# Filling the second half's row regions with pad rows inside the attention loop, ten block places a tile

## The reference

```
x = x + attention(layernorm(x), key, value, adj)     # x: 4096 x 512, adj: 4096 x 4096 of 0 and 1
x = x + experts(layernorm(x))                         # 8 experts of 512 x 512, the best 2 for each row

attention: q = x Wq' + bq; k = key Wk' + bk; v = value Wv' + bv
           s = (q k' / sqrt(4096)) * adj ; entries under 1e-5 in size become -1e9
           out = softmax(s) v Wm' + bm
experts:   gate = softmax(x Wg + bg); the two largest, scaled to sum 1
           out = sum over those two of gate * (We[e] x + be[e])
```

## Time and profile before

| | us |
|---|---|
| median of 3 runs | 1821.15 |
| the runs | 1818.61 to 1823.14 |
| the profiled execution | 1816.43 |
| its span | 1814.7 |
| PE busy | 1785.6 (98%) |
| DVE busy | 1201.1 (66%) |
| ACT busy | 743.6 (41%) |
| POOL busy | 242.8 (13%) |

### The profile page before, as it was taken

How to read it: one execution, slowest core, us unless ns; L and a number is a source line. 1 busy time by engine, 2 the same in 40 slices (tenths; PEclk the granted TensorE clock), 3 DMA queues, 4 the chain that set the end, 5 groups by cost and what they waited for, 6 DMA issues and landing times.

```text
span 1814.7 us, 33108 instructions
## 1 busy us (share of the span) xinstructions
PE 1785.6 (98%) x8770; PEld 838.5 (46%) x8770; DVE 1201.1 (66%) x3200; ACT 743.6 (41%) x1445; POOL 242.8 (13%) x285
## 2 busy tenths in 40 slices
PE   8999999999999999999999999999999999899997
PEld 3455444444444444444444444444444444445553
DVE  6888766666666666666767666666666665465453
ACT  4444444444444434444443333333334443233343
POOL 2000000000000000000000000000000000145654
PEclk9999999999999999999999999999999999999999
DMA  6555455776667776666776655565555667899986
GB/s 210 167 189 188 156 134 137 163 171 164 162 169 165 162 168 156 166 158 156 169 165 163 152 144 136 140 139 135 134 139 131 145 156 174 201 308 240 185 157 82
DMA packets 428619, 296.63 MB, mean 163 GB/s; under 512 B 319249, under 2 KB 335633, under 8 KB 428562
## 3 DMA queue, kind: packets, MB, share of 16 engines
q1 hardware_dynamic: 389810, 230.36, 51.6%
q0 software_dynamic: 16864, 38.35, 10.9%
q10 hardware_dynamic: 21888, 27.27, 5.0%
HBM read 152.68 MB, written 67.72 MB: 121 GB/s over the span
## 4 chain that ended last, share of the span: by engine, by line
PE 91%; DVE 3%; issue 3%; DMA 1%; ACT 1%; POOL 1%; DVEq 0%; ACTq 0%; SPq 0%; POOLq 0%
PE ps L1466 18%; PE ps L1467 18%; PE ps L1468 18%; PE ps L1579 12%; PE ps L1580 12%; PE ps L1581 12%; PE ps L1651 1%; PE ps L1523 1%; DMA slots<-work,slots_u 1%; DVE work L1418 1%; PE ps L1589 0%; DVE work L1410 0%; ACT work L910 0%; POOL out L640 0%; DVEq L1414 0%
## 5 line engine op out<-in xcount | busy, mean ns | idle before, releaser
L1466 PE MATMUL ps<-key_region,work 128*128 128x512 f16 (+1 forms) x1336 | 506.9, 379 | 4.0 <-issue 2.5
L1467 PE MATMUL ps<-key_region,work 128*128 128x512 f16 (+1 forms) x1336 | 506.8, 379 | 0.0
L1468 PE MATMUL ps<-key_region,work 128*128 128x512 f16 (+1 forms) x1336 | 506.7, 379 | 0.0
L780 ACT ACTIVATE work<-work 128x512 f32<-128x512 f32 x256 | 161.3, 630 | 566.7 <-DVE work L1090 566.3
L1579 PE MATMUL ps<-val_region,work 128*128 128x512 f16 x1024 | 388.9, 380 | 4.0 <-DMA work<-work 2.8
L1580 PE MATMUL ps<-val_region,work 128*128 128x512 f16 x1024 | 389.1, 380 | 0.0
L1581 PE MATMUL ps<-val_region,work 128*128 128x512 f16 x1024 | 389.0, 380 | 0.0
L1090 DVE SCALAR_TENSOR_TENSOR work<-ps,r_cur,work 128x512 f32<-128x512 f32 x256 | 191.7, 749 | 147.5 <-PE ps L1468 133.2
L1112 DVE TENSOR_TENSOR work<-work 128x512 f16<-128x512 f32 x256 | 176.4, 690 | 71.9 <-ACT work L793 71.8
L1100 DVE CUSTOM_DVE_ANT_0 work<-work 128x512 f32<-128x512 f32 x256 | 177.3, 692 | 49.5 <-DVE work L1097 49.5
L788 ACT ACTIVATE work<-work,exp_bias 128x512 f32<-128x512 f32 x256 | 181.4, 709 | 61.2 <-DVE exp_bias L1108 54.6
(11 more groups left out here) (200 smaller groups left out, 1594.4 us busy)
## 6 DMA issues: line engine op xcount, KB each, us to landing
work<-in_adj SPq DMA_DIRECT2D x256, 256.0 KB, 2.9
val_region<-slots SPq DMA_DIRECT2D x58, 257.0 KB, 5.2
work<-in_valueT SPq DMA_DIRECT2D x8, 1024.0 KB, 6.7
work<-in_x SPq DMA_DIRECT2D x8, 1024.0 KB, 5.2
work<-in_keyT SPq DMA_DIRECT2D x8, 1024.0 KB, 5.5
q_scratch<-work SPq DMA_DIRECT2D x8, 1024.0 KB, 5.1
work<-q_scratch SPq DMA_DIRECT2D x32, 256.0 KB, 2.7
work<-in_x SPq DMA_DIRECT2D x32, 256.0 KB, 3.0
```

What stands on the lines that cost most here:

```text
L780: nc.scalar.activation(w[:, c * CW:(c + 1) * CW], s_adj[:, c % 2, :], ACT.Abs).then_inc(abs_done, 1)
L1466: nc.tensor.matmul(bank, st[0], mv[0], start=(k == 0), stop=False)
L1467: nc.tensor.matmul(bank, st[0], mv[1], start=False, stop=False)
L1468: last = nc.tensor.matmul(bank, st[1], mv[0], start=False, stop=(k == n - 1))
```

## The change

`slots[1]` gets 160 blocks instead of 137, and all of it is filled with pads ahead of the scatters into it. In iterations 2 to 17 SP issues ten more transfers of one block each: two after adjacency chunk 7 and two after each of the transposes 4 to 7. The eight pads of the second half behind the tables go, and with them the wait for them; in its place SP waits for the tables. POOL waits for all 160 fills before it scatters the first row of the second half. The setup transfers that wrote the second half's spare block now go to an unused place of `slots[0]`.

```diff
+    FILL = 10
+    assert FILL * TH > DUMMY + 2 and FILL % 5 == 0
...
-        slots = [nc.dram_tensor(f"slots{h}", ((DUMMY + 1) * P, ROW), F32, kind="Internal").ap() for h in range(HALVES)]
+        slots = [nc.dram_tensor(f"slots{h}", (FILL * TH * P, ROW), F32, kind="Internal").ap() for h in range(HALVES)]
...
+            def fill_slots(t, i):
+
+                for j in range(2):
+                    sp.dma_start(slots[1][bass.ds(t * (FILL * P) + (2 * i + j) * P, P), :], pad_row[:, :]).then_inc(filled, 16)
...
                 adjacency(t, 7)
+                if h == 0:
+                    fill_slots(t - 2, 0)
                 for c in range(ADJ, C):
                     turn_probs(t - 1, c)
+                    if h == 0:
+                        fill_slots(t - 2, c - ADJ + 1)
                     if not last and c < C - 1:
                         adjacency(t + 1, c - ADJ)
...
             def pad_regions(h):
 
+                if h:
+                    return
                 sp.wait_ge(tables_done, h + 1)
...
             pad_regions(1)
             sp.wait_ge(slotted, 32 * T)
-            sp.wait_ge(padded[1], 16 * E)
+            sp.wait_ge(tables_done, 2)
             for st in rest:
                 load_block(st)
...
-                    nc.gpsimd.dma_start(slots[h][DUMMY * P + q * rows:DUMMY * P + (q + 1) * rows, :], pad_row[part, :]
+                    nc.gpsimd.dma_start(slots[0][(DUMMY + 2 * h) * P + q * rows:(DUMMY + 2 * h) * P + (q + 1) * rows, :], pad_row[part, :]
                                         ).then_inc(y_added[8 * h + 2 * q + 1], 16)
...
                 scatter_rows(t, 0)
+            pool.wait_ge(filled, 16 * FILL * TH)
             with pool.Fori(TH, T - 2) as t:
```

More of the change, by code:

```diff
@@ L372, in graph_attention_moe_kernel @@
         padded = [sem(f"padded{h}") for h in range(HALVES)]
+        filled = sem("filled")
         tok_loaded = [sem(f"tok_loaded{b}") for b in range(TOKS)]
```

## The result

| | before | after |
|---|---|---|
| median of 20 runs each, us | 1819.32 | 1823.85 |
| lowest to highest | 1813.17 to 1823.38 | 1819.87 to 1832.46 |
| ratio after to before | | 1.0028, 95% interval 1.0019 to 1.0038 |
| span of the profiled execution | 1814.7 | 1822.6 |

The change makes the kernel slower by about 5.1 us (0.28%, interval 3.5 to 6.9 us). That is just inside the 0.3% that the prediction called no change, and outside zero: with 20 runs of each the difference shows.

What follows compares the result with a forecast made beforehand. The prediction took PE to bound the kernel from end to end. Its terms, 0 - 0 + 0.4 = +0.4 us, added to the expected median 1821.15, gave 1821.5 us, range 1817 to 1831.

Steps and rivals of the forecast that it cites:

- The step to 0 in fifteen iterations: Attention loop: q lands 4.1 us after issue, at most 4.3, PE needs it at 4.61; cost 0 in fifteen iterations.
- The hole in SP's queue has 8 us of cover: Block stage: the block loaded after the late pads arrives 8.0 us before PE turns it; removing the pads gains 0.
- The load of q is the transfer with the least room, 4.61 us from issue to use: Loop: q, issued at 644.25 and used at 648.86, decides the cost; other transfers behind the fills have more room.
- Two fills ahead are 1.4 us of data: Loop: the pair behind transpose 7 takes 2 x 0.70 = 1.4 us, with q's data behind it.
- It isn't delayed: SP after transpose 7: two fills take about 1 us, end at about 643.75, and q still goes at 644.25.
- At most 4.3 us: Loop: upper landing of q after issue in fifteen iterations, 2.9 + 1.4, against PE's need at 4.61.
- A share of 0.86: Transfer engines in the loop's iterations with fills: the share goes from 0.69 to 0.86.
- 0.4 us once, in the first iteration: First iteration: q lands at 3.6 + 1.4 = 5.0 us, so PE waits 0.4 us once.
- ACT's weight pieces are covered: Loop, another queue: a piece comes 1.4 us late behind a fill pair, DVE's need is 1.8 us after; no cost.
- Rival A: Loop: q late in every tile, landing after 5.2 us; PE waits 0.6 us in 16 tiles, 9.6 us, 1831; chance 0.20.
- Rival B: Block stage: the removed hole and traffic end PE's 4.4 us of "issue" waits and more; 1815.5 to 1817; chance 0.06.
- Rival C: Fills are issued later than placed and POOL waits for them, costing only past 987; chance under 0.01.

Runs made afterwards that it cites:

- The pair alone: Kernel before with its eight late pads, plus only the fill pair behind transpose 7 (32 fills); ratio 1.0007 to the kernel before.
- 8 bytes a row: Kernel before with late pads and only the pair behind transpose 7, each transfer writing 2 of 514 columns; ratio 1.0000 to before.
- The run with two pairs: Changed kernel with the pair from behind adjacency chunk 7 also moved behind transpose 7, four fills ahead of q; ratio 1.0287 to the kernel before.
- the pair behind q: Changed kernel, all 160 fills, with the last pair issued behind the load of q and last adjacency chunk; ratio 0.9998 to the kernel before.

## Why the prediction was right or wrong

The time, 1823.85 us, lies in the range, and "within 0.3%" holds by a hair. That is in part luck. The forecast was a change of +0.4 us and it is about +5.1; the forecast's 1821.5 us looks closer to the result because it stood on a median of three runs, 1821.15, where twenty give 1819.32. The step to 0 in fifteen iterations doesn't hold: the loop loses 0.2 to 0.4 us in each. Of the prediction's own signs for being wrong, iterations of 42 us or more are there in the first trace (42.08), and half of its loads of q land after 4.6 us or more. By its own steps:

- *The hole in SP's queue has 8 us of cover*: right. Without it PE's "issue" waits are 5.2 us in place of 4.4, so nothing is won, and with the pads kept beside the fills the time is the same within the noise.
- *The load of q is the transfer with the least room, 4.61 us from issue to use*: right. PE's only new wait is for it.
- *Two fills ahead are 1.4 us of data*: the size is right, the mechanism half right, and that they agree is luck. The pair alone moves the landing from 2.7 to 4.2 and 4.1 us; with 8 bytes a row it is 2.8. But about half of it is data, and the other half is q's landing, which follows the second fill's by 0.2 us. The prediction had this wait in its hands: it put the confirmation of the fills at 648.5, 4.25 us after q's issue, found it "still ahead of 648.86" and left the landing of q at 4.1. Measured, the second fill lands 4.0 us after q's issue with the pair alone, 4.4 and 4.1 in the two traces of the changed kernel.
- *"It isn't delayed" (the issue of q)*: wrong, and half of the miss or more. I took two direct transfers at 0.34 + 0.1 us each, the rows of single transfers on a quiet SP. The pairs behind transposes 5 and 6 do take 0.95 and 0.90 us, but the one behind transpose 7 takes 1.4 (median, 1.5 at most; why is not shown), and q is issued 0.5 us late (median, 0.6 at most). I had the other price, 1.03 us each from the pads, and argued it away with "q stands behind the fills' data until later anyhow". The run with two pairs shows that issue and data add.
- *"At most 4.3 us"*: wrong by up to 1.0. With all ten fills q takes 4.0 to 5.3 us in one execution and 3.6 to 4.8 in another. The late issue and the landing make 0.5 + 4.5 = 5.0 and 0.5 + 4.3 = 4.8 us against 4.61: 0.4 and 0.2 us over, and the iterations are 0.39 and 0.18 us longer. I had taken the fills' price in a stretch where SP's queue carried little else.
- *A share of 0.86*: it is 0.91 in the first trace and 0.88 with the pair behind q. By the queue's totals from 300 to 940 the packets of SP took 78.5% in place of 56.2% for some 154 fills: 0.223 x 640 / 154 = 0.93 us a fill, not 0.70. Whether the fills' packets or those beside them grew is not told apart.
- *0.4 us once, in the first iteration*: there is such a wait, of 1.4 us at most, and it is not the only one.
- *ACT's weight pieces are covered*: right in what counts. ACT now waits for their loads, 13.3 us in all and 1.4 at most, but with the pair behind q it does so too (13.8 us) and the time is that of before.
- *Rival A* had the right mechanism and the wrong size, 9.6 us: it needed a landing of 5.2 us in every tile. *Rival B* shows nothing measurable. *Rival C*: POOL did not wait for the fills.

The Trainium skill's rule (DMA: Bandwidth & Descriptors, "Queues, rings and completion order"), that a ring's descriptors are consumed in order, is what the runs show: the same fills behind q are free. Its second part, a completion that lands only after every earlier write of that engine, agrees with the traces as well: with full rows ahead q lands 0.19 us behind the second fill and about 0.7 us later than its own packets would have it, with 8 bytes a row it is 0.1 us late at most.

## What to carry to other kernels

Before filling a queue's idle time, find the transfer on it with the least room between landing and use, and put the filler behind that one; the same 160 transfers cost 5 us with two of each ten directly ahead of that load and nothing with the two behind it. Price a filler by the terms that add: the issuing engine's time, the data ahead on the queue, the landing of the writes ahead, and what else is still in the queue. Both bursts cost far more than the same fills spread out, one on SP's queue and one on POOL's. A cover that the sum leaves at 0.3 us isn't a cover: the landings of one trace spread over 1.2 us. And where PE is made to wait long, add what its clock then costs.

## What the runs showed of the hardware

- The pair of direct transfers behind transpose 7 holds SP for 1.4 us whether it carries 2056 or 8 bytes a row; the pairs behind transposes 5 and 6 take 0.95 and 0.90 us, single ones 0.34.
- A load directly behind two writes of 257 KB on the same queue lands 0.19 us behind the second write (median, in both traces of the changed kernel and of the pair alone), although its own last packet started 1 us earlier; without the pair it lands 0.3 us behind that packet.
- A burst of ten blocks issued by POOL made a transpose on SP's queue take 8.7 to 13.8 us to land (3.3 us is the rule without it), and its issue 3.4 us in the median: traffic of one queue is felt in the issue on another.
- At a share of 0.88 and 223 GB/s of mixed transfers PE ran 679.98 of 680 us at the full granted clock. Where it waited longest, in the runs with the fills from POOL and in the first stage, the mean granted clock of the execution was 0.981 and 0.974 against 0.997: 0.96 in the loop of the one, 0.82 from 80 to 320 us of the other, where PE was busy in 152 of 240 us.
